# The last four turns by their angles, cut into three parts each and spread over twelve periods of attention

## The reference, cut to what matters

```
q = rope((layernorm(x) @ wq) per head)        # 32 heads of 128
k, v = rope(ctx @ wk), ctx @ wv                # 8 heads of 128, four query heads share one
w = softmax(mask(q k^T / sqrt(128)))
x = x + tanh(g) * (concat(w v) @ wo)
```

## Time and profile before

| | us |
|---|---|
| median of 3 runs (range) | 3019.99 (3018.98 to 3020.39) |
| profiled execution, its own time | 3022.68 |
| its span, first to last instruction | 3020.9 |
| TensorE matmuls busy | 2964.4 (98%) |
| TensorE weight loads busy | 2484.8 (82%) |
| VectorE busy | 2025.8 (67%) |
| ScalarE busy | 1283.2 (42%) |
| GpSimd busy | 1368.0 (45%) |

### The profile page before, as it was taken

How to read it: one execution, slowest core, us unless ns; L and a number is a source line. 1 busy time by engine, 2 the same in 40 slices (tenths; PEclk the granted TensorE clock), 3 DMA queues, 4 the chain that set the end, 5 groups by cost and what they waited for, 6 DMA issues and landing times.

```text
span 3020.9 us, 41023 instructions
## 1 busy us (share of the span) xinstructions
PE 2964.4 (98%) x14656; PEld 2484.8 (82%) x14656; DVE 2025.8 (67%) x4714; ACT 1283.2 (42%) x2686; POOL 1368.0 (45%) x1104
## 2 busy tenths in 40 slices
PE   9999999999999999999999999999999999999999
PEld 7888878887788878887888788888888888888887
DVE  4432478888655686679667777666776676666566
ACT  4111366665422422242224555655555544454332
POOL 2422378896322577778776333322322311111254
PEclk9999999999999999999999999999999999999999
DMA  7332421212555654455444676676667556665531
GB/s 248 129 119 98 175 59 49 78 63 74 197 174 177 195 158 111 112 156 155 112 109 132 210 263 226 223 252 202 197 207 253 182 189 205 205 200 165 223 110 72
DMA packets 320661, 488.29 MB, mean 162 GB/s; under 512 B 26236, under 2 KB 155644, under 8 KB 317644
## 3 DMA queue, kind: packets, MB, share of 16 engines
q1 hardware_dynamic: 319740, 484.23, 50.0%
q10 hardware_dynamic: 720, 1.44, 0.1%
HBM read 324.12 MB, written 161.48 MB: 161 GB/s over the span
## 4 chain that ended last, share of the span: by engine, by line
PE 57%; DVE 5%; ACT 1%; DMA 1%; issue 0%; POOL 0%; SPq 0%; ACTq 0%; DVEq 0%
PE PB L150 18%; PE PB L152 18%; PE PB L151 18%; PE PB L2375 3%; DVE qp_b L2132 1%; DVE qp_r L2169 0%; PE PB L2800 0%; DVE at_ptl L2514 0%; DVE PB L2172 0%; DVE at_ss L2494 0%; DVE qp_r L2177 0%; ACT at_ss L2422 0%; DVE qp_c L2174 0%; DMA qp_raw<-in_wq 0%; DVE qp_r L2170 0%
## 5 line engine op out<-in xcount | busy, mean ns | idle before, releaser
L2537 POOL TENSOR_TENSOR at_ql<-at_qf,at_qh 128x512 fp32r<-128x512 f32 x128 | 166.5, 1301 | 855.3 <-ACT at_qh L2415 855.3
L2422 ACT ACTIVATE at_ss<-at_ss,at_sm,at_bs 128x256 f32<-128x256 f32 x512 | 301.9, 591 | 337.3 <-DVE at_sm L2498 337.3
L150 PE MATMUL PB<-at_woh,at_ah 128*128 128x512 f32 x1024 | 400.6, 391 | 1.7 <-POOL at_wol L2544 1.0
L151 PE MATMUL PB<-at_wol,at_ah 128*128 128x512 f32 x1024 | 399.9, 391 | 0.0
L152 PE MATMUL PB<-at_woh,at_al 128*128 128x512 f32 x1024 | 399.3, 390 | 0.0
L2528 DVE SCALAR_TENSOR_TENSOR at_xt<-PB,gt,at_xt 128x512 f32<-128x512 f32 x256 | 192.0, 750 | 254.1 <-PE PB L152 254.1
L150 PE MATMUL PB<-qp_b,qp_a 128*128 128x512 f32 x896 | 351.2, 392 | 6.7 <-DVE qp_r L2175 3.7
L151 PE MATMUL PB<-qp_b,qp_a 128*128 128x512 f32 x896 | 349.9, 391 | 0.0
L152 PE MATMUL PB<-qp_b,qp_a 128*128 128x512 f32 x896 | 349.8, 390 | 0.0
L2199 POOL TENSOR_TENSOR qp_a<-qp_raw,qp_a 128x512 fp32r<-128x512 f32 x192 | 259.8, 1364 | 100.9 <-ACT qp_a L2094 98.2
L2094 ACT ACTIVATE qp_a<-qp_raw 128x512 fp32r<-128x512 f32 x192 | 113.2, 625 | 295.1 <-POOL qp_raw L2203 163.6
(11 more groups left out here) (309 smaller groups left out, 7583.1 us busy)
## 6 DMA issues: line engine op xcount, KB each, us to landing
at_woh<-wod SPq DMA_DIRECT2D x48, 1024.0 KB, 6.9
at_wol<-wod SPq DMA_DIRECT2D x48, 1024.0 KB, 9.4
qp_raw<-in_wq SPq DMA_DIRECT2D x32, 1024.0 KB, 5.3
qd<-qp_r SPq DMA_DIRECT2D x256, 128.0 KB, 2.5
at_qf<-qd SPq DMA_DIRECT2D x128, 256.0 KB, 3.3
at_rawo<-in_wo SPq DMA_DIRECT2D x32, 512.0 KB, 6.0
wod<-at_woh SPq DMA_DIRECT2D x16, 1024.0 KB, 5.4
wod<-at_wol SPq DMA_DIRECT2D x16, 1024.0 KB, 6.6
```

Source lines behind the costliest of these rows:

```text
L150: pe.matmul(o, ah, bh, start=start, stop=False)
L151: pe.matmul(o, ah, bl, start=False, stop=False)
L2422: m = act.activation(at_ss[s][:, c, :], at_ss[s][:, c, :], ACT.Exp, bias=z[:, 4 + c:5 + c], scale=at_bs[:, qn % 2, 8 + 2 * b + c % 2:9 + 2 ...
L2537: self.pool.tensor_tensor(at_ql[n % 3][:, :], at_qf[n % 2][:, :], asf(at_qh[n % 3][:, :]), ALU.subtract).then_inc(*inc("at_pool", ("q", n)))
```

## The change

`turn` gets an argument `part`. On VectorE part 0 is L2169 and L2170 with the waits ahead of them, part 1 is L2172 and L2174, part 2 is L2175 and L2177. SyncE's four stores of a turn are issued with part 2. For all pairs but the last two, the three parts follow each other directly, which is the order of before. For pairs 30 and 31 there is a pause behind each part: twelve parts of two operations stand ahead of periods 6 to 17, one ahead of each. `at_schedule` pauses behind its first 18 periods. The operations are the same, in number, shape and place.

```diff
                     if i > 4 and block[-1] < LASTP:
                         for pair in block:
-                            do.turn(pair, i - 5)
+                            for part in range(3):
+                                do.turn(pair, i - 5, part)
...
             for tn in range(2):
                 for pair in Q_BLOCKS[-1]:
-                    yield
-                    do.turn(pair, tn)
-                    yield
+                    for part in range(3):
+                        do.turn(pair, tn, part)
+                        yield
...
-            def turn(self, pair, tn):
+            def turn(self, pair, tn, part):
...
+                if part == 0:
+                    on.wait_ge(*at("qp_rope", 1))
+                    on.wait_ge(*at("qp_dve", ("sum", pair, (5, 6)[tn])))
+                    if n > 1:
+                        on.wait_ge(*at(f"qp_s{n % 2}", Q_TURNS[n - 2] + (1, 1)))
+                    else:
+                        on.wait_ge(*at("f0_xos", (NT // 2 - 1, 5)))
+                    dve.tensor_tensor(q0, top, qp_angle(0, tn), ALU.mult)
+                    dve.tensor_tensor(q1, top, qp_angle(1, tn), ALU.mult).then_inc(*inc("qp_dve", ("top", pair, tn)))
+                if part == 1:
+                    on.wait_ge(*at("qp_dve", ("top", pair, tn)))
+                    dve.tensor_tensor(top, low, qp_angle(1, tn), ALU.mult).then_inc(*inc("qp_dve", ("sine", pair, tn)))
+                    on.wait_ge(*at("qp_dve", ("sine", pair, tn)))
+                    dve.tensor_tensor(low, low, qp_angle(0, tn), ALU.mult).then_inc(*inc("qp_dve", ("low", pair, tn)))
+                if part == 2:
+                    dve.tensor_tensor(q0, q0, top, ALU.subtract).then_inc(*inc("qp_dve", ("q0", pair, tn)))
+                    on.wait_ge(*at("qp_dve", ("low", pair, tn)))
+                    dve.tensor_tensor(q1, q1, low, ALU.add).then_inc(*inc("qp_dve", ("q1", pair, tn)))
...
-            def turn(self, pair, tn):
+            def turn(self, pair, tn, part):
+                if part < 2:
+                    return
                 sp, on, h, n, sb = self.sp, self.on, 2 * (pair % NP), Q_TURNS.index((pair, tn)), pair // NP
...
-                if u < 14 or WF <= u < WF + 48 or u > NU - 2:
+                if u < 18 or WF <= u < WF + 48 or u > NU - 2:
                     yield
```

More of the change, by code:

```diff
@@ L2162, in turn @@
                     qp_sum(pair, (4, 6)[tn]), qp_sum(pair, (5, 3)[tn]), qp_r[n % 2][0][:, :], qp_r[n % 2][1][:, :]))
[L2163 to L2176, removed]
@@ L2177, in turn @@
-                dve.tensor_tensor(q1, q1, low, ALU.add).then_inc(*inc("qp_dve", ("q1", pair, tn)))
+                if part == 0:
[7 more added lines that the diff above has]
+                    dve.tensor_tensor(q1, top, qp_angle(1, tn), ALU.mult).then_inc(*inc("qp_dve", ("top", pair, tn)))
```

## The result

The changed kernel takes 3027.13 us (median of 15 runs, 3024.22 to 3032.20), the kernel before 3019.59 us (15 runs, 3014.18 to 3021.90): 7.5 us more where 7.6 were forecast. In these runs the kernels' ranges don't overlap. The ratio is 1.0028, 95% interval 1.0020 to 1.0035.

A forecast was written before the change was run, and what follows sets the result against it. TensorE, busy 98% of the span, bounds the kernel. Eleven rounds (7 x 10.84 + 4 x 10.96 = 119.7 us) put period 20 7.6 us later, costs beside it 0: 3019.99 + 7.6 = 3027.6 us, range 3015 to 3031.

The forecast's parts named there:

- The port wait: VectorE operations with both inputs in SBUF wait until a running GpSimd operation ends; each part's second operation starts 0.48 us behind.
- (a): Rival: no port wait matters, parts only delay `at_ptl` by 0.82 us; loss 4.2 us instead of 11.83, 3012.3 us; chance 0.11.
- (b): Rival: only part 0 of each turn waits for GpSimd; loss 7.5 us, 3015.7 us; chance 0.13 with its variants.
- The order: In each delayed period the part comes 0.28 us behind the start of GpSimd's `at_wol` and waits some 2 us.
- (c): Rival: the part slips ahead of `at_wol` by the 0.28 us it lacks; 17.8 us of loss, 3026 us; chance 0.07.
- The ring: From `at_ptl` through `at_wol` and the next part back to `at_ptl`: 10.84 us a round, 10.96 with part 1, against TensorE's 9.14.
- The sum: Eleven rounds of 119.7 us put the head of period 20 at 1822.5 against 1814.91: 7.6 us later.
- the clock: TensorE's clock is full and added waits of 0.6 to 2.6 us resemble those of before (1.41): cost 0.
- the 4.2 that the working allows: `at_ptl` must start by T + 4.22 us, T the period's head, 0.83 ahead of the values due at T + 5.05.
- the slack of 2.95 us: Time `at_ptl` can slip before TensorE waits: starts at T + 1.27, needed at T + 4.22; covers one round's loss of 1.7 to 1.8.

The follow-up runs named there:

- stats_at_head: Changed kernel with the six operations of a turn for pairs 30 and 31 made bn_stats of one SBUF input, same places; 3010.5 us, ratio 0.9971 to the kernel before.
- parts_behind_maxima: Changed kernel with the twelve parts behind the shift (L2506) of periods 6 to 17 instead of ahead of them; 3008.4 us, ratio 0.9960 to the kernel before.
- parts_every_second: Changed kernel with the twelve parts ahead of the odd periods 7 to 29 instead of 6 to 17; 3013.0 us, ratio 0.9979 to the kernel before.
- one_input: Changed kernel with the six operations of a turn for pairs 30 and 31 made multiplications of one SBUF operand by 0.5; 3022.5 us, ratio 1.0004 to the kernel before.
- the second comparison: The changed kernel run again as it is, for a second trace, against the kernel before; 3025.1 us, ratio 1.0019.
- whole_behind_maxima: Kernel before with its whole turns of six operations behind the shift of periods 7, 9, 11, 13 instead of ahead; 3020.9 us, ratio 1.0004 to the kernel before.

## Why the prediction was right

**The port wait** held in all twelve parts, not only in part 0: L2171, L2175 and L2179 in their SBUF forms last 1.5 to 2.7 us: 1.5 in period 6, 1.8 in period 12, where the clock had fallen in the period ahead and the part came later, and 2.6 to 2.7 in the others. That GpSimd holds them, and not the place, is shown by stats_at_head (same place, no wait) and parts_behind_maxima (other place, no wait). Rivals (a) and (b) fell with the trace after. But (a)'s price was right: where nothing waits (stats_at_head), the loss is 3.9 us where it said 4.2.

**The order** of part and `at_wol`, by 0.28 us, is 0.27 in the rows above. Rival (c) did not come.

**The ring** was put at 10.84 to 10.96 us; it is 10.83 from part 1 to part 2, and the eleven rounds forecast at 119.7 us took 119.37. parts_every_second shows that it needs successive periods, one_input that its length follows the length of a part.

**The sum**: +7.6 us forecast, +8.3 and +7.2 in the two traces' stretches, +7.5 and +5.4 in the medians. Both stretches lie within the +6.5 to +8.7 that the working gave, and neither within its narrower +7.3 to +8.1. That the first median comes within 0.1 us of the forecast is partly luck: it holds a term that the sum had at 0, and the second comparison gives +5.4. That lies under the 6.0 us that I had called distinguishable, but its interval, 1.0010 to 1.0029, does not include 1.

**The term that was wrong**: the clock, put at 0 because the added waits were "like those of before". They are longer (2.38 us against 1.41) and come in every second period, and TensorE's clock halved for 3.2 to 3.4 us twice in each of the two traces. The ring hid three of the four; the fourth explains most of the 1.2 us that the first trace has over the second. The trace of before had a warning, outside the stretch that I had read: behind a wait of 1.94 us for the weights, in the work on the mask, the granted clock fell there as well (TensorE's timeline, and a stretch with the columns given above):

```profile
1871.85 2.12 PE L2375 MATMUL PB<-idt,at_ss 128*128 128x128 f32 x8 [1.94 <-DVE at_ss L2508]
...
1871.85:1875.00 3.15, 3.15 (x14) 2.82 (x15) 2.99 (x7) 1.20 (x2) 0.00 (x0) 0.58 0.59 215
```

**A reading that was wrong**: of TensorE's waits after, I said that none would be on `at_ptl`. Some 0.6 us in even periods are (2.3 us in four), because there `at_ptl` comes 5.0 us into the period, beyond the 4.2 that the working allows; the length (0.6 to 0.8 us was forecast for even periods) was right, the cause was not. Those on `at_wol`, put at 13 us with 2.6 each, are 12.1 with up to 2.4.

**What was read too narrowly**: that an operation waits for GpSimd if both its inputs are in SBUF. Operations with one input at doubled rate wait as well, and so do the weights. In the sum it changed nothing; it made two expectations too low (one_input, whole_behind_maxima).

## What to carry to other kernels

Before work is spread over periods, ask what else runs at the chosen point of each period: a piece that fits VectorE's idle time can still wait for GpSimd, if both work in SBUF alone; and if GpSimd's next operation hangs on what stands behind the piece, the waits join into a ring whose length, not the amount of work, sets the pace. Add the durations round the ring and compare them with the bound engine's period: here 10.84 against 9.14 us gave the sign, and with the slack of 2.95 us the size. Then look for the point where the other engine is idle, and check that the work pushed behind the piece doesn't meet it either.

## What the runs showed of the hardware

A wait of VectorE for GpSimd stands inside the duration of the waiting operation and shows as busy time, not as a wait (VectorE's busy time rose from 2025.8 to 2034.9 us with the same instructions). In parts_every_second all twelve such operations end 0.54 to 0.56 us behind GpSimd's. Float32 operations that waited: 128x512 with two inputs in SBUF (680 ns alone), 128x512 with one input at doubled rate (411 ns alone), and 128x256 multiplied by a column (340 ns alone, up to 1575). Not waiting: `bn_stats` of 128x512 with one input in SBUF (675 to 695 ns in 24), and L2174 with an operand in PSUM (698 to 700 ns in 54, at least 35 of them started while a GpSimd operation ran).

GpSimd may wait in its turn: in whole_behind_maxima the `at_wol` that starts before the turn's last operation has ended lasts 2.65 to 2.66 us in all four turns, where 2.39 is usual. No run isolates that.

The granted clock of TensorE halved behind four of the seven waits of 2.3 to 2.4 us in the changed kernel's two traces, at a different period each time; what decides between them stays open. So it does for shorter ones: none of five waits of 2.0 to 2.2 us in one_input was followed by a fall, one of four of 2.2 us in whole_behind_maxima was.
